# A decoder layer: value products of self-attention in column strips, cross-attention with in-place exponentials and transposed value products

## The reference, cut to what matters

```python
# self-attention: 4 branches of 16 heads of 32; the scores outside a band of the branch are 0,
# a sink logit with a null value is added, the branches are averaged
w = scores / denom * full_mask
probs = softmax(concat([w, tanh(sink)]))
out = probs[..., :T] @ v + probs[..., T:] * v_nulls
y = (out_as_ctx @ WO + bO).mean(over the 4 branches)
# cross-attention: 16 heads of 32, the softmax over the 32 largest of 722 scores only
scores = q @ k.T / sqrt(32)
top_scores, top_idx = top_k(scores, 32)
out = softmax(top_scores) @ v[top_idx]
# feed-forward: real(ifft(fft(x) @ w)) + bias, a product with one 512x512 matrix
```

## Time and profile before

| | |
|---|---|
| median of 3 runs | 2798.91 us (2797.72 to 2809.83) |
| span of the profiled execution | 2800.8 us |
| PE busy | 2418.1 us, 86% |
| DVE busy | 2028.2 us, 72% |
| ACT busy | 1388.0 us, 50% |
| POOL busy | 1016.6 us, 36% |

### The profile page before, as it was taken

The page is one execution under the profiler, slowest core; times in us unless marked ns, Lnnn a source line. Parts: engine busy times, 40 slices in busy tenths (PEclk is TensorE's granted clock), DMA queues, the critical chain, the costliest instruction groups (busy, mean ns, idle before and its releaser), DMA issues. The chain is left out here.

```text
span 2800.8 us, 41238 instructions
## 1 busy us (share of the span) xinstructions
PE 2418.1 (86%) x13752; PEld 1992.5 (71%) x13752; DVE 2028.2 (72%) x3897; ACT 1388.0 (50%) x2992; POOL 1016.6 (36%) x912
## 2 busy tenths in 40 slices
PE   3899999999999757898898989888988988988987
PEld 2667767776776536777777868777777877877875
DVE  4544544454454206899898899998989989998996
ACT  3221122112212025667667666766767667676663
POOL 3344334433533112343343343333434433333421
PEclk9787788788878678999999999999999999999987
DMA  4000000000000220010010000000001001000000
GB/s 157 7 18 9 9 17 9 9 9 18 9 9 6 84 86 25 12 28 14 16 28 14 15 20 23 15 20 23 14 16 28 14 16 28 14 16 23 14 1 7
DMA packets 37615, 63.00 MB, mean 22 GB/s; under 512 B 4014, under 2 KB 20542, under 8 KB 37420
## 3 DMA queue, kind: packets, MB, share of 16 engines
q1 hardware_dynamic: 35836, 56.28, 6.7%
q0 software_dynamic: 1584, 4.30, 0.5%
HBM read 53.99 MB, written 6.55 MB: 22 GB/s over the span
## 5 line engine op out<-in xcount | busy, mean ns | idle before, releaser
L1208 DVE MATCH_REPLACE8 ca_W<-ca_top,ca_W 128x722 f32<-128x722 f32 (+1 forms) x624 | 553.5, 894 | 0.0
L1199 DVE MAX8 ca_top<-ca_W 128x8 f32<-128x722 f32 (+1 forms) x624 | 536.4, 898 | 2.6
L855 POOL TENSOR_TENSOR ca_E<-ca_E,ca_S 128x722 f32<-128x722 f32 (+1 forms) x208 | 357.6, 1740 | 308.6 <-ACT ca_S L1060 308.5
L955 PE MATMUL ca_pO<-ca_V,ca_PT 128*128 128x64 f32 (+1 forms) x2496 | 343.1, 293 | 76.8 <-ACT ca_ctxT L1099 76.5
L955 PEld LDWEIGHTS ca_pO<-ca_V,ca_PT 128*128 128x128 f32 (+1 forms) x2496 | 331.1, 205 | 103.8 <-ACT ca_PT L1082 75.6
L837 POOL TENSOR_TENSOR ca_KL<-ca_K,ca_KH 128x384 fp32r<-128x384 f32 (+1 forms) x128 | 114.2, 893 | 496.5 <-ACT ca_KH L1053 496.5
L618 PE MATMUL sa_pq<-sa_V,sa_E 101*100 101x33 f32 x1536 | 258.9, 355 | 29.2 <-POOL sa_E L341 27.8
L618 PEld LDWEIGHTS sa_pq<-sa_V,sa_E 101*100 101x100 f32 x1536 | 257.2, 287 | 30.0 <-issue 30.0
L383 ACT ACTIVATE sa_V<-sa_pp 100x512 f32<-100x512 f32 x48 | 29.2, 608 | 461.1 <-PE sa_pp L90 410.7
L845 POOL TENSOR_TENSOR ca_cL<-ca_raw,ca_cH 128x768 fp32r<-128x768 f32 (+1 forms) x64 | 110.6, 1728 | 332.8 <-ACT ca_cH L1036 332.8
L1187 DVE MAX8 ca_top<-ca_S 128x8 f32<-128x722 f32 (+1 forms) x208 | 181.2, 901 | 54.3 <-ACT ca_S L1077 48.7
(11 more groups left out here) (193 smaller groups left out, 5252.1 us busy)
## 6 DMA issues: line engine op xcount, KB each, us to landing
ca_raw<-in_ctxT SPq DMA_DIRECT2D x32, 384.0 KB, 3.7
ca_raw<-in_ctxT SPq DMA_DIRECT2D x32, 338.0 KB, 3.0
sa_xin<-in_x SPq DMA_DIRECT2D x16, 200.0 KB
sa_xres<-in_x SPq DMA_DIRECT2D x16, 200.0 KB
x_scratch<-sa_x SPq DMA_DIRECT2D x16, 200.0 KB
ca_xin<-x_scratch SPq DMA_DIRECT2D x16, 200.0 KB
out<-ca_x SPq DMA_DIRECT2D x16, 200.0 KB
sa_E<-in_WQ SPq DMA_DIRECT2D x12, 256.0 KB, 13.5
```

The costliest lines, as they stand in the source:

```text
L855: pool.tensor_tensor(E[r][0:t.rows, :], E[r][0:t.rows, :], S[r][0:t.rows, :], ALU.subtract).then_inc(p_ready, 1)
L955: last = pe.matmul(out, PT[:, k, 0:t.rows], rhs, start=k == 0, stop=k == KC - 1)
L1199: n_of[t.i] = order.mark(dve.max(eight, w[rows, :]))
L1208: ins = dve.match_replace(w[rows, :], eight, (w if k else S[r])[rows, :], REMOVED)
```

## The change

In self-attention the value products are turned round. First come 48 matmuls that add up the denominators: a stationary matrix of 32 columns (`picker`) puts the sum for head and branch into one of 32 partitions, and the weights (100 columns) move; four heads write to four column strips. Then 48 with V (32 columns) stationary and the weights moving give the numerators, features on the partitions, again in four column strips. DVE takes one reciprocal; in the next pass, after the value projection of branch 0, 48 matmuls of 32 by 32 spread the reciprocals over the partitions, ACT copies them out, DVE multiplies and adds, and the four transposes of the context go away. DVE's reciprocal stands before its wait for POOL's powers.

In cross-attention there are four W buffers and no E: the exponentials are taken in place, in S and in W, and POOL subtracts in S. The value product has V (32 columns) stationary and the transposed weights moving, one matmul per head that the tile touches, each in its column strip; the reciprocal sums, broadcast as a stationary operand against the identity, give the denominators in the same layout. ACT copies both once per group of three tiles (`keep_output`), POOL multiplies (`place_output`). Shift, reciprocal (a power) and the low part of the queries move from DVE to POOL. The work on the next batch's input moves from step 4 to step 3; the queries' high parts move to the end of step 5 on ACT. PE's order in a step becomes: first score tile, projections of part 0, first `weights_T`, the odd jobs, projections of part 1, first `values`, second score tile, second `weights_T`, second `values`. On ACT, each `keep_scores` stands behind the `keep_weights_T` of the tile whose S buffer it takes over.

```diff
+        pick = sb("pick", [T + 1, 64 + DH])
+        rden, rb = sb("rden", [128, T]), sb("rb", [128, NL, CC * T])
+        ctxT = rb[:, 0, :].rearrange("p (c q) -> p c q", c=CC)
...
+        def picker(c):
+
+            return pick[:, 64:64 + DH] if c == 0 else pick[:, DH - 1 - c:2 * DH - 1 - c]
+
+        def spread(c, k):
+
+            at = DH * k + c
+            return ident[DH * k:DH * k + DH, at:at + 1].broadcast_to((DH, DH))
+
+        rb_bank = [pq[:, 3, T:T + CC * T], pt[:, 0:CC * T], pw[:, 0:CC * T]]
...
+                    if br == 0 and prev:
+
+                        need(act, y_mm, b.count(1, -1))
+                        for n in range(NL):
+                            act.wait_ge(rb_mm, b.count(HK * NL, HK * (n + 1 - NL)))
+                            act.activation(rb[:, n, :], rb_bank[n], ACT.Copy).then_inc(rb_ready, 1)
...
+                    dve.wait_ge(den_mm, b.count(HK, HK))
+                    dve.reciprocal(rden[:, :], pq[:, 3, 0:T]).then_inc(rden_ready, 1)
...
-                    dve.wait_ge(roped, b.count(1, 1))
-                    dve.wait_ge(pv_mm, b.count(1, 1))
...
-                    t5 = tmp[:, :].rearrange("p (h n d) -> p n h d", h=NH, n=NL)
-                    c3 = heads(ctxr[:, :], NH)
-                    then(dve.tensor_tensor(c3, t5[:, 0], t5[:, 1], ALU.add))
-                    dve.tensor_tensor(c3, c3, t5[:, 2], ALU.add).then_inc(ctx_ready, 1)
+                    dve.wait_ge(num_mm, b.count(HK, HK))
+                    for n in range(NL):
+                        dve.wait_ge(rb_ready, b.count(NL, n + 1))
+                        dve.tensor_tensor(rb[:, n, :], pq[:, n, 0:CC * T], rb[:, n, :], ALU.mult).then_inc(num_used, 1)
+                    dve.wait_ge(num_used, b.count(NL, 2))
+                    order.mark(dve.tensor_tensor(rb[:, 0, :], rb[:, 0, :], rb[:, 1, :], ALU.add))
+                    third = rb[:, 2, :].rearrange("p (c q) -> p c q", c=CC)
+                    dve.wait_ge(out3_ready, b.count(1, 1))
+                    dve.wait_ge(num_used, b.count(NL, 3))
+                    then(dve.tensor_tensor(third, third, out3[:, :].unsqueeze(2).broadcast_to((128, CC, T)), ALU.add))
+                    dve.tensor_tensor(rb[:, 0, :], rb[:, 0, :], rb[:, 2, :], ALU.add).then_inc(ctx_ready, 1)
...
-                    if br == 1 and prev:
-                        pe.wait_ge(ctx_ready, b.count(1, 0))
-                        for c in range(CC):
-                            last = pe.transpose(pt[:, T * c:T * c + T], ctxr[:, 128 * c:128 * c + 128], ident[0:T, 0:T])
-                        last.then_inc(cT_mm, 1)
+                    if br == 0 and prev:
+                        pe.wait_ge(rden_ready, b.count(1, 0))
+                        pe.wait_ge(out3_ready, b.count(1, 0))
+                        settle(pe)
+                        for n in range(NL):
+                            for g in range(CC):
+                                for k in range(HK):
+                                    rows = slice(DH * k, DH * k + DH)
+                                    last = pe.matmul(rb_bank[n][rows, T * g:T * g + T], spread(NL * g + n, k),
+                                                     rden[rows, :], start=True, stop=True)
+                                    if g == CC - 1:
+                                        last.then_inc(rb_mm, 1)
...
-                    for h in range(NH):
-                        for br in range(NL):
-                            at = ((h % HK) * NL + br) * (DH + 1)
-                            last = pe.matmul(pq[0:T, h // HK, at:at + DH + 1], E[0:T + 1, h, br, :], V[:, h, br, :],
+                        pe.wait_ge(pick_ready, 1)
+                    for c in range(CAP):
+                        g, n = divmod(c, NL)
+                        for k in range(HK):
+                            last = pe.matmul(pq[DH * k:DH * k + DH, 3, 0:T], picker(c), E[0:T + 1, HK * g + k, n, :],
+                                             start=c == 0, stop=c == CAP - 1)
+                            if c == CAP - 1:
+                                last.then_inc(den_mm, 1)
+                    for c in range(CAP):
+                        g, n = divmod(c, NL)
+                        for k in range(HK):
+                            h = HK * g + k
+                            last = pe.matmul(pq[DH * k:DH * k + DH, n, T * g:T * g + T],
+                                             V[0:T + 1, n, DH * h:DH * h + DH], E[0:T + 1, h, n, :],
                                              start=True, stop=True)
-                    last.then_inc(pv_mm, 1)
+                            if c == CAP - 1:
+                                last.then_inc(num_mm, 1)
...
+            def shifts(tb, tp, t):
+                r, rows = ring(t, tp), slice(0, t.rows)
+                pool.wait_ge(peaked, tb.count(NT, t.i + 1))
+                settle(pool)
+                pool.tensor_scalar(shift[rows, r:r + 1], top[r][rows, 0:1], -SCALE, None,
+                                   ALU.mult).then_inc(shift_ready, 1)
+
+            def weights(tb, tp, t):
+                r, rows = ring(t, tp), slice(0, t.rows)
+                ob, oi = before(tb, t, RING)
+                pool.wait_ge(e_ready, tb.count(NT, t.i + 1))
+                pool.wait_ge(f_ready, tb.count(NT, t.i + 1))
+                pool.tensor_tensor(S[r][rows, :], S[r][rows, :], W[r][rows, :], ALU.subtract).then_inc(p_ready, 1)
+                need(pool, o_mm, parts_done(ob, Tile(oi)))
+                pool.wait_ge(z_ready, tb.count(NT, t.i + 1))
+                pool.tensor_tensor(rZ[rows, r:r + 1], Z[rows, r:r + 1], minus_one[rows, :], ALU.pow).then_inc(rz_ready, 1)
+
+            def place_output(tb, tp, t):
+
+                n = group_of(t)
+                if n is None or t.rest:
+                    return
+                if n == 0:
+                    need(pool, y_mm, tb.count(1, 0))
+                pool.wait_ge(o_kept, tb.count(GROUPS, n + 1))
+                pool.tensor_tensor(ctxT[:, n, :], NR[:, 0, :], NR[:, 1, :], ALU.mult).then_inc(ot_ready, 1)
...
+                at = T * (t.g % 2)
+                for _, cols, to, g, q in t.blocks():
+                    pe.matmul(pO[to:to + DH, DEN + at + q.start:DEN + at + q.stop],
+                              rZ[:, r:r + 1].broadcast_to((128, DH)), ident[:, cols], start=True, stop=True)
                 for k in range(KC):
-                    if t.rest:
-                        rhs = V[tp][:, k, :].rearrange("p (g h d) -> p g h d", g=4, h=4)[:, :, 3, :]
-                    else:
-                        h = 4 * t.g + t.t
-                        rhs = V[tp][:, k, DH * h:DH * h + t.dims]
-                    out = pO[0:t.rows, 0:t.dims]
-                    if t.rest:
-                        out = out.rearrange("p (g d) -> p g d", g=4)
-                    last = pe.matmul(out, PT[:, k, 0:t.rows], rhs, start=k == 0, stop=k == KC - 1)
-                last.then_inc(o_mm, 1)
-
-            def output_T(tb, tp, t):
-                pe.wait_ge(o_ready, tb.count(NT, t.i + 1))
-                settle(pe)
-                pe.transpose(pO[0:t.dims, 256:256 + t.rows], On[0:t.rows, 0:t.dims],
-                             ident[0:t.rows, 0:t.rows]).then_inc(ot_mm, 1)
+                    for _, cols, to, g, q in t.blocks():
+                        last = pe.matmul(pO[to:to + DH, NUM + at + q.start:NUM + at + q.stop],
+                                         V[tp][:, k, 128 * g + to:128 * g + to + DH], PT[:, k, cols],
+                                         start=k == 0, stop=k == KC - 1)
+                        if k == KC - 1:
+                            last.then_inc(o_mm, 1)
...
                 for s in range(7):
                     cur, last, coming = tiles_at(s, b, par, tiles, prev, nxt)
+                    if coming:
+                        score(*coming[0])
+                    for x in slices(s, 0, b, par, tiles, nxt):
+                        project(*x)
+                    if last:
+                        weights_T(*last[0])
...
                     for x in slices(s, 1, b, par, tiles, nxt):
                         project(*x)
                     if last:
-                        weights_T(*last[0])
-                    for x in late_tile(s, b, par, tiles, prev):
-                        output_T(*x)
-                    if s < 6 and len(coming) > 1:
+                        values(*last[0])
+                    if len(coming) > 1:
                         score(*coming[1])
...
+            def exps(tb, tp, t):
                 r, rows = ring(t, tp), slice(0, t.rows)
+                act.wait_ge(removed, tb.count(NT, t.i + 1))
+                act.wait_ge(shift_ready, tb.count(NT, t.i + 1))
+                act.activation(S[r][rows, :], S[r][rows, :], ACT.Exp, bias=shift[rows, r:r + 1],
+                               scale=SCALE).then_inc(e_ready, 1)
+
+            def keep_scores(tb, tp, t):
                 ob, oi = before(tb, t, RING)
```

(42 more changed lines are left out.)

312 lines of the change are left out of this document (139 added, 173 removed).

## The result

The changed kernel takes 2980.54 us (median of 4 runs, 2980.01 to 2984.79) against 2804.37 us for the kernel before on the same chip: 1.0618 times as long, 95% interval 1.0582 to 1.0653. It is slower, as forecast, but by 176 us where the forecast had some 40, and outside the range.

The account below looks back on a forecast made before the run. PE was busy 86% of the span, with DVE nearly as full in cross-attention; the question was which engine the others wait for. 2800.8 - 12 (self-attention) + 52 (cross-attention) = 2841 us, say 2840; range 2700 to 2925.

Parts of the forecast that it names:

- The -12: Self-attention's term in the sum: 15 batches at -0.8 us each.
- the prediction's last rival: Column strips don't run beside each other: about +17 us a self-attention batch, near 3100 us in all; chance 0.06.
- The switch of tiling mode: PE between whole array and strips: some 0.1 us each, 2.6 us a cross-attention batch, left out of the sum.
- The hand schedule of the shorter batch: Step-by-step count of one shorter cross-attention batch: 108.7 us against 102.4 before, +6.3 us.
- M to D: Cross-attention, DVE's end of step 0's second maximum to the start of step 4: 59.6 us, before 56.0.
- D to M: Cross-attention, start of step 4 to DVE's end of the next step 0's second maximum: 49.1 us, before 46.4.
- the turn: Cross-attention, passage to the next batch: query projection's end to step 0's second maximum, 17.2 us against 12.7.
- M: Cross-attention, moment DVE ends its second maximum of step 0; forecast 17.2 us after the query projection.
- the upper bound: Cross-attention, +8 us a batch: clock at half after the 4.6 us idle, `values` one at a time.
- The longer batches: Cross-attention batches 4.4 us longer on average, with more room for added waits; so +3.5 us carried, not +6.3.
- DVE's waits are all for the score copies: Cross-attention sign: largest at step 0 (8 to 10 us in two pieces), 2 us at steps 2 and 5.
- The first rival: Cross-attention: turn hidden, DVE's work decides, 2717 or 2660 us; holds if the turn takes under 10 us; chance 0.32.

Follow-up runs that it names:

- e10: Changed kernel with odd jobs, slices, score tiles, rest tile, shifts and reciprocals reordered, queries' high parts in step 6, low parts on DVE; 2785.69 us, ratio 0.9929.
- l1: e10 with the transposed input and the spectral product again behind the first `weights_T`; 2843.12 us, ratio 1.0142.
- e3: Changed kernel with output product, transposed input and spectral product ahead of the step's first score tile on PE; 2977.89 us, ratio 1.0637.
- e9: Changed kernel with the queries' high parts on ACT in step 6 and their low parts back on DVE; 2965.15 us, ratio 1.0562.

## Why the prediction was right in its sign and wrong in its size

**Self-attention: right.** Strips run four at a time, the clock is at half for the denominators (4.0 forecast, 3.96 measured) and full for the numerators (2.0, 2.25), the spreading waits for `out3` (6.7 us forecast, 6.82 measured), and the period falls by 0.43 us instead of 0.8. The stage gained 19 us, not 12: I multiplied the period by 15 and didn't look at the last batch. The -12 lay near only because two errors went against each other: too much per batch, and nothing for the last one. By the factor for three column tiles in the prediction's last rival, its 2.0 us comes to 2.5 us, not 2.6 to 2.8; 2.25 were measured.

**The switch of tiling mode: small.** From the last denominator to the first numerator and on to V nothing stands out in the timeline. e10 has all the strips and all the switches, and its period is 107.5 us against 107.0 in the kernel before. So the drain that the Trainium skill ("TensorEngine Tiling (Array Packing)", Key Properties) states for a change of tiling mode is at most a small term here.

**DVE's work: right,** 94.5 us forecast, 94.2 measured; by busy time 4.3 us less a batch, 4.8 forecast.

**The hand schedule of the shorter batch: 108.7 us forecast, 116.2 measured** (2020.3 to 2136.5). This is the failed step: PE's order was priced with the odd jobs of steps 1 and 4 at nothing, and at full clock. By DVE's waits in the rows above:
- M to D is 62.3 us instead of 59.6. The score copy of step 2 costs 3.79 instead of 1.9, the sum behind the output product (L1302) costs 0.39 instead of nothing; the rest tile's 1.45 is near the 1.2.
- D to M is 53.9 instead of 49.1. The sum behind the spectral product (L1291) waits 3.62, forecast nothing; the score copy of step 5 waits 0.31 instead of 1.9, since DVE comes late itself; the turn waits 9.37 + 3.03 = 12.4, forecast 8 to 10.

These are DVE's waits; what sets M is the chain on PE. There D to M splits into 34.0 us to the end of the query projection (2116.65, 31.9 forecast) and 19.8 from there to M (17.2 forecast). Of the first 2.1 us, 2.0 are there when PE leaves step 4 (at 2102.0, 19.4 us into it, 17.4 forecast).

The cause of that, and of the late copies in step 2: the sum for steps 1 and 4 let PE go from the first weights' transposition to the key slices, held only by the context split at 8.4. The odd jobs `L1071` and `L1079` stand between. Eight records at the 0.43 us that I had used elsewhere make 3.4 us, and after standing 4.58 and 5.31 us PE takes 5.29 and 4.42 for them. The key slices of step 4 start at 2092.50, 9.9 us into the step, where the forecast had 8.4; POOL ends the context split at 8.9, so about 0.5 of the 1.5 us are POOL's and 1.0 the odd job's. l1 shows that the place of the later two jobs costs 3.8 us a period when nothing else hides it; e3 shows that mending it alone brings nothing, as PE then stands for the context split and runs the key slices at half clock.

The turn was placed well (PE stands 5.15 us ahead of the first score tile, 4.6 forecast; M comes 19.8 us after the query projection, 17.2 forecast, 12.7 before). Of the 2.6 us, 0.6 are POOL's low parts (4.52 us for four, forecast 0.96 each). The rest is the clock: the term took full clock, and the score tile and half of the slice run at half, 2.0 and 4.1 us instead of 1.1 and 2.8. Half clock stood only in the upper bound.

**The longer batches: they absorbed nothing.** The short batch alone gave +6.3 us by my sum, and I carried +3.5, because DVE, with less work, would have room in the longer ones. No row bore that. By the timelines, from M to M, the changed kernel's batches take 116.2 and 122.8 us in turn. Those of the kernel before, from its fourth period on, take 102.4 to 106.9 (six, mean 104.8) and 106.8 to 112.2 (five, mean 109.0). So the shorter kind lost 11.4 and the longer 13.8, and the 102.4 that I followed was the shortest of all, not a typical one. The rest tile's wait, 1.2 us in my sum, is 51.2/12 = 4.3 us on the average. Of the 142 us between 2841 and the span of 2983, this cut is 15 x 2.8 = 42; the schedule's own error is the larger part, 15 x (12.7 - 6.3) = 96.

**"DVE's waits are all for the score copies"** fell: of the 25.3 us a period they are 199.0/12 = 16.6; 4.3 are the rest tile's, 3.8 the spectral product's, 0.7 the output product's.

**The first rival,** that the turn is hidden and DVE's work decides, fell in the kernel as changed, by its own point of 10 us against 19.8. How much of the whole loss is the clock was not isolated; single stretches show its price, 2.3 us on e3's two key slices and about 2 on the turn's score tile and slice. The windows from 1300 to 2600 us give 0.89 granted in the changed kernel, 0.95 in the kernel before and 0.93 in e10; that it is low because PE stands, and so follows the orders, is argued and not shown. That the exponentials share their buffers with scores and weights was not tested by itself; e10 has it too.

## What to carry over

Before you cut work from the busiest engine, list for each step every instruction queued on the engines that feed it, the odd jobs too, and price them at the clock the feeder will have after its wait. When several chains end within a few us of each other, undoing one can show nothing or little (e3 0, e9 0.9 us a period); mend them together and then take one back at a time (3.8, 4.1 and 5.7). The self-attention half gained 19 us; the cross-attention half was no gain even in the best order found: e10 is as fast as the self-attention half alone (0.9929 and 0.993).

## What the runs showed of the hardware

Four column strips ran wholly beside each other in fp32: 48 products of 100 columns in 2.25 us, where 12 rounds of four passes at 2.4 GHz are 2.0, and in 3.96 us at half clock, where they are 4.0. And where PE has stood 4 to 5 us in this kernel, it works for some microseconds at the 1.2 GHz level, so that a wait costs more than its own length: eight records of 512 columns took 5.29 and 4.42 us there, and 3.68 and 3.59 us in the kernel before (from 1732.97 and 1775.22).
